# Vision tower on one core: the last stage in token x channel form behind the attention projection

## The chip, the cores and the metric

The kernel runs on one core of one Trainium2 chip. The metric is device time in microseconds; several executions are taken and their median is compared.

## What is computed

Four images of 3138 tokens with 128 channels (3136 patches of 4 x 4 and two class tokens) go through four blocks, each fed by a layer norm and added to its input. The change lies in the last two:

```python
h = h + _L1_attn_ref(_layernorm(h), w_qkv, w_proj, b_proj)   # windows of 64 tokens; per token an 8 x 8 softmax over its heads
h = h + _L1_ffn_ref(_layernorm(h), ln_scale, ln_bias, ...)
# _L1_attn_ref, last step: out.transpose(0, 2, 1, 3).reshape(B*nw, W, C) @ w_proj.T + b_proj
# _L1_ffn_ref:
flat = norm(flat) * ln_scale + ln_bias
out_shared = swiglu(flat @ shared_in_w.T) @ shared_out_w.T + shared_out_b
g_idx = argmax(flat @ group_gate_w.T + group_bias)           # one of 2 groups
topv, topi = top_k(softmax(e_logits of that group), 2)       # two of its 4 experts
h_expert = swiglu(flat @ expert_in_w.T)                      # one hidden layer of 256 for all experts
routed = cnt @ expert_out_bias
for e in range(8):
    routed = routed + comb[:, e:e+1] * (h_expert @ expert_out_weight[e].T)
return out_shared + routed
```

The transpose before the projection mixes tokens and heads inside a window, so a row of the projection's input comes from eight tokens. All of it is float32; the shares and counts are split into bf16 pieces where they pass TensorE.

## The kernel before

Three phases follow each other, each with a hand-written program for every engine; a wait is always on a semaphore. Phase A (patches, norm, state-space scan, first norms) and phase B (for each of 8 experts the 1024 best tokens, by a radix search on DVE, then gather, two matmuls and a scatter back into `h_rows`) are all but untouched. Phase C holds the last two blocks.

Phase C works on 25 groups of 512 tokens. A group passes five stages, one in each turn: L (load and row norm), A (q, k, v and the head softmax), N (projection and second norm), U (up projections and gates), X (experts). `group_turns` runs 29 turns, so in a full turn five groups are in work, and in the first and last four only some of them. Each engine has one list of steps for a turn, written out by hand at the end of `tensor` (L1710 to L1746), `scalar` (L1851 to L1872), `vector` (L2051 to L2080), `gpsimd` and `sync`. `BANK_ORDER` (L1420) gives each result of TensorE one of eight PSUM banks; `result` waits for the matmul, `taken` waits until the bank was emptied.

What a turn does:

- **A**: TensorE turns `n3`, then four matmuls make q, k and v (L1645), which ACT copies out (`qkv_copy`). POOL multiplies q with k (L2089, four of 1024 elements) and, after the softmax, the probabilities with v (L2096). DVE sums the products (`sum_scores` L1964, `sum_values` L1991) and forms the softmax (`less_top`, `probs`). The value sums of tiles 2 and 3 run in the next turn.
- **N**: TensorE turns the attention result `o` (`turn_o`, L1653), ACT copies it to `ot` (`keep_o`, L1790), SP writes it to DRAM (`heads`, L1586) and reads it back dealt out anew by eight DMAs (`dealt`, L1589). `project` (L1691) has the result as channel x token and adds the token rows `x` through four matmuls with the identity (L1695). Mean and variance run over the partitions, so they are matmuls too: `center` and `variance`. ACT and DVE finish the norm (`keep_h3`, `square`, `column_scale`, `rescale`, `affine`).
- **U**: eight up matmuls (L1613), `silu` on ACT and `hidden` on DVE give `hid`. `gates` (L1629) and nine small DVE operations (`choose_group`) pick the group.
- **X**: `choose_experts` (L2023 to L2047, 16 small DVE operations and four writes into `cc`) makes counts and shares. They are turned, split into three bf16 pieces on ACT and DVE (`keep_choice`, `split_mid`, `middle_choice`, `split_low`) and spread over the partitions by `spread` (L1672, one bf16 matmul of 512 columns per expert). DVE multiplies both halves of the hidden layer by them:

```python
dve.tensor_tensor(sc[:, k % SC_RING, :, :], hid[X % 2][:, 2:4, :],
                  tile_of(f"cb{e}", X)[:].unsqueeze(1).to_broadcast([P, 2, GW]), ALU.mult)   # scale, L1957, 1024 elements
```

and `expert` (L1680) adds two matmuls per expert into the bank ACC, where `shared` and `biases` already are. `finish` (L1900) adds the residual, and SP stores the group.

SP's list for a turn is: load `x` three groups ahead, store the last result (it waits for `finish`), then `heads` out and `dealt` in. Its weights for phase C are loaded at the start of the phase (L1573, L1574).

## Time and profile before

| | us |
|---|---|
| median of 3 runs | 2853.29 |
| lowest, highest | 2849.75, 2855.03 |
| profiled execution, own time | 2854.72 |
| its span from first to last instruction | 2852.9 |
| first weight load of phase C | 1819.9 |
| PE, DVE busy | 2417.9 (85%), 2351.7 (82%) |
| POOL, ACT busy | 1946.2 (68%), 1544.7 (54%) |
| mean granted TensorE clock | 0.934 of 2.4 GHz |

The span and the runs' times differ by under 2 us. Phase A takes about the first 1480 us, phase B until 1820, phase C the rest, some 1033 us. PE, DVE, ACT and POOL are the compute engines, SP issues DMAs. A wait is listed with the instruction that ended it. Durations of neighbouring instructions overlap a little, so start-to-start distances are shorter than the durations beside them: two DVE sums of 1024 elements take 2.33 together and 1.22 each.

### The profile page before, as it was taken

What the parts mean: (1) busy time and instruction counts of PE and PEld (TensorE: products, weight loads), DVE (VectorE), ACT (ScalarE), POOL (GpSimd) and SP (SyncE); (2) the same over time, 40 slices, a digit from 0 to 9 for tenths busy, and PEclk for the clock granted to TensorE, in tenths of its full rate; (3) what the DMA queues carried; (4) which work ended last, traced back from release to release, by engine and by line L of the source; (5) the groups of instructions that cost most, each with busy time, mean ns of one, the idle gap of its engine ahead of it and who ended that gap; (6) DMA issues with size and microseconds to landing.
All of it is one profiled execution on the core that took longest, in us unless ns stands there. A gap on an engine that the chain in (4) does not pass through costs nothing. (4 is left out here: it accounts for less than half of the span.)

```text
span 2852.9 us, 25309 instructions
## 1 busy us (share of the span) xinstructions
PE 2417.9 (85%) x6774; PEld 1128.9 (40%) x6774; DVE 2351.7 (82%) x3447; ACT 1544.7 (54%) x2598; POOL 1946.2 (68%) x1008
## 2 busy tenths in 40 slices
PE   5999999999999999999861397159999999899988
PEld 2444444444444444444321143024444444444443
DVE  2999999999999999999978522158887888888875
ACT  4777777777776777777632153134344444344332
POOL 2898898988989889898950388565555555555540
PEclk8999999999999999999975598559999999999999
DMA  2333433334333333433320043300101000011000
GB/s 75 101 120 92 124 105 113 108 95 123 103 112 106 104 118 100 124 98 110 114 82 0 20 70 56 57 22 26 30 30 30 26 28 24 26 30 30 26 23 11
DMA packets 169759, 199.28 MB, mean 70 GB/s; under 512 B 38969, under 2 KB 156946, under 8 KB 169490
## 3 DMA queue, kind: packets, MB, share of 16 engines
q1 hardware_dynamic: 158354, 189.27, 21.6%
q0 software_dynamic: 11264, 8.40, 2.2%
q8 instruction: 56, 0.92, 0.1%
q14 instruction: 85, 0.70, 0.1%
HBM read 164.37 MB, written 33.25 MB: 69 GB/s over the span
## 5 line engine op out<-in xcount | busy, mean ns | idle before, releaser
L915 POOL TENSOR_TENSOR a_hc<-a_h,a_cs 128x896 f32<-128x896 f32 (+1 forms) x448 | 859.5, 1938 | 55.8 <-DVE a_h L778 55.6
L362 PE MATMUL a_y_bank<-a_hc,a_ident 128*128 128x448 f32 (+1 forms) x1792 | 741.8, 544 | 21.8 <-DVE a_yz L798 21.2
L553 ACT ACTIVATE a_da<-a_dt,a_neg_a 128x448 f32<-128x448 f32 (+1 forms) x896 | 551.9, 631 | 296.0 <-DVE a_h L778 291.0
L778 DVE TENSOR_TENSOR_SCAN a_h<-a_da,a_h,a_dbx 128x448 f32<-128x448 f32 x528 | 582.9, 1133 | 9.5 <-ACT a_da L553 4.4
L2096 POOL TENSOR_TENSOR c_prod<-c_prob,c_qkv 128x1024 f32<-128x1024 f32 x100 | 280.8, 2848 | 272.2 <-DVE c_prob L1983 272.2
L362 PEld LDWEIGHTS a_y_bank<-a_hc,a_ident 128*128 128x128 f32 x1792 | 331.5, 190 | 326.3 <-issue 272.6
L1680 PE MATMUL c_p_ACC<-c_sc,c_w_ex 128*128 128x512 f32 x800 | 363.7, 592 | 0.0
L762 DVE TENSOR_TENSOR a_dbx<-a_dtx,a_b_bank 128x896 f32<-128x896 f32 (+1 forms) x308 | 327.3, 1063 | 16.2 <-PE a_b_bank L355 16.1
L2089 POOL TENSOR_TENSOR c_prod<-c_qkv 128x1024 f32<-128x1024 f32 x100 | 231.8, 2341 | 153.2 <-ACT c_qkv L1764 153.2
L1957 DVE TENSOR_TENSOR c_sc<-c_hid,c_p_CB 128x1024 f32<-128x1024 f32 x200 | 240.0, 1214 | 68.5 <-PE c_p_CB L1672 65.8
L903 POOL TENSOR_TENSOR a_dbp<-a_dtx,a_bs 128x896 f32<-128x896 f32 (+1 forms) x140 | 270.9, 1935 | 0.0
L778 DVE TENSOR_TENSOR_SCAN a_h<-a_da,a_h,a_dbp 128x448 f32<-128x448 f32 x240 | 263.1, 1128 | 0.0
L1680 PEld LDWEIGHTS c_p_ACC<-c_sc,c_w_ex 128*128 128x128 f32 x800 | 151.7, 190 | 182.0 <-issue 179.4
L1613 PE MATMUL c_p_W<-c_fl,c_w_up 128*128 128x512 f32 x400 | 211.3, 624 | 9.5 <-ACT c_fl L1848 8.2
L1758 ACT ACTIVATE c_act_half<-c_p_W 128x512 f32<-128x512 f32 x100 | 59.9, 599 | 251.0 <-PE c_p_W L1613 248.9
L405 PE MATMUL a_work<-a_xn,a_w_tap 128*128 128x448 f32 (+1 forms) x448 | 187.3, 552 | 3.7 <-ACT a_xn L694 3.7
L355 PE MATMUL a_b_bank<-a_bc,a_sel 128*128 128x448 bf16 (+1 forms) x308 | 110.2, 358 | 73.5 <-DVE a_dbx L762 71.5
L1385 POOL DMA_INDIRECT b_xg<-n_rows,b_index x64 | 62.3, 974 | 141.2 <-DVE b_tab L1255 122.0
L1991 DVE TENSOR_REDUCE c_o<-c_prod 128x128 f32<-128x1024 f32 x100 | 117.2, 1211 | 38.7 <-POOL c_prod L2096 38.7
L1964 DVE TENSOR_REDUCE c_score<-c_prod 128x64 f32<-128x1024 f32 x100 | 121.2, 1212 | 20.2 <-POOL c_prod L2089 18.0
L932 POOL TENSOR_TENSOR a_spl<-a_spl,a_yt 128x896 f32<-128x896 f32 (+1 forms) x28 | 58.6, 2094 | 90.3 <-DVE a_yt L805 68.0
L1764 ACT COPY c_qkv<-c_p_T 128x384 f32<-128x384 f32 x100 | 49.0, 490 | 130.7 <-PE c_p_T L1645 123.1
(304 smaller groups left out, 3718.2 us busy)
## 6 DMA issues: line engine op xcount, KB each, us to landing
a_cs<-c_rows SPq DMA_DIRECT2D x96, 896.0 KB, 5.2
a_bs<-c_rows SPq DMA_DIRECT2D x24, 1120.0 KB, 5.6
a_cs<-c_rows SPq DMA_DIRECT2D x16, 900.0 KB, 4.4
c_x<-h_rows SPq DMA_DIRECT2D x25, 256.0 KB, 2.7
heads<-c_ot SPq DMA_DIRECT2D x25, 256.0 KB, 2.3
c_dealt<-heads SPq DMA_DIRECT2D x200, 32.0 KB, 1.9
rolled<-c_res SPq DMA_DIRECT2D x25, 256.0 KB, 2.1
h_rows<-a_th SPq DMA_DIRECT2D x24, 224.0 KB
```

Of the source, the lines that this page charges most:

```text
L362: pe.matmul(y_bank[:, d, 0:g.w], ident[:], hc[:, (g.i * NS + n) % HC_RING, d, 0:g.w], start=(n == 0), stop=(n == NS - 1)).then_inc(s_sum, 1)
L405: mm = pe.matmul(tile_of(use, p)[:, 0:w], w_tap[:, j, d * P:(d + 1) * P], xn[:, j:j + w], start=(j == 0), stop=(j == KC - 1))
L553: act.activation(da[:, k % DA_RING, 0:g.w], dt[g.slot][:, d, 0:g.w], ACT.Exp, scale=neg_a[:, d * NS + n:d * NS + n + 1]).then_inc(s_da, 1)
L762: dve.tensor_tensor(dbx[:, k % DBX_RING, :, 0:g.w], dtx[g.slot][:, :, 0:g.w], b_bank[:, 0:g.w].unsqueeze(1).to_broadcast([P, 2, g.w]), ALU ...
L778: dve.tensor_tensor_scan(h[:, n, d, 0:g.w], da[:, (g.i * 2 * NS + k) % DA_RING, 0:g.w], x, state, ALU.mult, ALU.add).then_inc(s_scan, 1)
L903: pool.tensor_tensor(dbp[:, k % DBP_RING, :, 0:g.w], dtx[g.slot][:, :, 0:g.w], bs[:, POOL_STATES.index(n), 0:g.w].unsqueeze(1).to_broadcas ...
L915: pool.tensor_tensor(hc[:, (q.i * NS + n) % HC_RING, :, 0:q.w], h[:, n, :, 0:q.w], cs[:, n % C_RING, 0:q.w].unsqueeze(1).to_broadcast([P, ...
L1613: end(f"up{m}", U, pe.matmul(p[:], w_up[:, m * P:(m + 1) * P], fl[U % 2][:], start=True, stop=True))
L1680: mm = pe.matmul(p[:], w_ex[:, i, e * D:(e + 1) * D], sc[:, k % SC_RING, i, :], start=False, stop=(e == E1 - 1 and i == 1))
L1957: dve.tensor_tensor(sc[:, k % SC_RING, :, :], hid[X % 2][:, 2:4, :], tile_of(f"cb{e}", X)[:].unsqueeze(1).to_broadcast([P, 2, GW]), ALU.mu ...
L2089: pool.tensor_tensor(prod[j][:].rearrange("p (h g d) -> p h g d", h=NH, g=NH), q.rearrange("p (h d) -> p h d", d=DH).unsqueeze(2).to_broad ...
L2096: pool.tensor_tensor(prod[j][:].rearrange("p (h d g) -> p h d g", h=NH, g=NH), prob[:, j * NH:(j + 1) * NH, :].unsqueeze(2).to_broadcast([ ...
```

## The change

Phase C keeps its five stages, groups and eight banks. From `project` on, everything is token x channel, with tokens on the partitions:

- `project` is one bf16 matmul for the bias and four float32 matmuls of 128 columns that have `dealt` as the stationary side. The residual is added by DVE (`add_rows`) from SBUF. Mean and variance come from `bn_stats` and `bn_aggr` on DVE, the scaling is four ACT instructions with a scale and a shift per row (`norm_rows2`), and TensorE turns the result (`turn_n2`) for the up matmuls. `center`, `variance`, `square`, `column_scale`, `rescale`, `keep_h3` and the identity matmuls go.
- `ex(n)` multiplies one tile of 128 tokens of the hidden layer, now the stationary side, with the weights of four experts at once, 512 moving columns; two of them cover a tile. There are still 16 matmuls of 512 columns in a turn. The shares, now one number per row, are applied as the two banks E0 and E1 are emptied: `by_act` (0 to 3) with four ACT instructions of 128 columns each, `by_dve` (4 to 7) with one DVE instruction of 512. `spread`, `scale` and both splits go. The bias matmul is four bf16 matmuls of 128 columns.
- POOL adds the two halves of each tile (`add_experts`, 512 elements, four per turn) between its products. DVE sums the four pairs, the residual and ACC in `total`, two `tensor_reduce` per group whose summed axis has a step of 128 elements. ACT copies ACC out (`keep_acc`).
- The windows are dealt so that a tile holds the same places of eight windows: `x` is loaded by four DMAs instead of one, `keep_o` writes runs of eight elements, and the output is token x channel.
- `qkv_copy(j)` waits for the value product of its own tile only. SP stores the last result after it has issued `heads`.
- The constants of phase C get their own memory beside phase B's and are loaded during it. POOL's fills at the start of phase B wait for DVE's first five operations there.

```diff
+            if e == 2:
+                progs["c_load"](sp)
             need(sp, s_out, 2 * (e - 1))
...
+            if r == 6:
+                progs["c_clear"](dve)
             decide(r, limit[0])
...
+        pool.wait_ge(s_dve, progs["n_high"])
         pool.memset(ones[:], 1.0).then_inc(s_fill, 1)
         pool.memset(zeros[:], 0).then_inc(s_fill, 1)
...
+    def load(sp):
+        for dst, name in ((k.ident, "ident"), (k.w_qkv, "w_qkv"), (k.w_proj, "w_proj"), (k.w_up, "w_up"),
+                          (k.w_gate, "w_gate"), (k.cols, "cols_c"), (k.w_so, "w_so"), (k.w_ex, "w_ex"),
+                          (k.earlier, "earlier"), (k.later, "later"), (k.pick, "picks_p")):
+            sp.dma_start(dst[:], a[name]).then_inc(k.s_in, 16)
+        sp.dma_start(k.gate_b[:], a["gate_b"].rearrange("o n -> (o n)").partition_broadcast(P)).then_inc(k.s_in, 16)
+        sp.wait_ge(k.s_const, 1)
+        for first in PARTS:
+            sp.dma_start(k.bias10[first:first + NBIAS, :], a["bias10"]).then_inc(k.s_in, 16)
...
+        free = result(eng, f"ex{n}", c)
+        rows = sc[:, entry % SC_RING, half * EG:(half + 1) * EG, :]
+        got = tile_of(f"ex{n}", c)[:].rearrange("p (e d) -> p e d", e=EG)
+        return rows, got, shares[:, c % 2, j, half * EG:(half + 1) * EG], free
+
...
+            def load():
+                if L is not None:
+                    if L >= 3:
+                        taken(sp, "proj", L - 3)
+                    rows = h_rows[L * GW + SHIFT:(L + 1) * GW + SHIFT, :].rearrange("(w n) d -> n w d", n=WIN)
+                    for j in range(GT):
...
+                    taken(sp, "o", N)
+                    sp.dma_start(heads[N % 2], ot[:]).then_inc(s_heads[N % 2], 16)
+
+            def heads_in():
...
+                        sp.dma_start(dealt[s][j * DH:(j + 1) * DH, :, :],
+                                     heads[s][:, j, :].rearrange("(h d) c -> d h c", d=DH)).then_inc(s_dealt[s], 16)
+
+            load()
...
+                    for j in range(GT):
+                        for k in range(2):
+                            pe.matmul(p[:, j * D:(j + 1) * D], hid[X % 2][:, k, j * P:(j + 1) * P], w_so[:, k, :],
+                                      start=(j == 0 and k == 0), stop=False, skip_group_check=True)
...
+                    for j in range(GT):
+                        mm = pe.matmul(p[:, j * D:(j + 1) * D], c_b[0:KB, j * P:(j + 1) * P], bias_b[0:KB, :],
+                                       start=False, stop=True, skip_group_check=True)
+                    end("acc", X, mm)
...
+                    j, half = n // 2, n % 2
+                    if n == 0:
+                        taken(pe, "up7", X)
+                    p = begin(f"ex{n}", X)
                     for i in range(2):
-                        mm = pe.matmul(p[:], w_ex[:, i, e * D:(e + 1) * D], sc[:, k % SC_RING, i, :], start=False,
-                                       stop=(e == E1 - 1 and i == 1))
...
+                        mm = pe.matmul(p[:], hid[X % 2][:, 2 + i, j * P:(j + 1) * P],
+                                       w_ex[:, i, half * EG * D:(half + 1) * EG * D], start=(i == 0), stop=(i == 1))
+                    end(f"ex{n}", X, mm)
...
+                    pe.matmul(p[:], pick_b[0:KB, :], bias_b[0:KB, :].unsqueeze(1).to_broadcast([KB, GT, D]),
+                              start=True, stop=False, skip_group_check=True)
...
                     for j in range(GT):
-                        mm = pe.matmul(p[:, j * P:(j + 1) * P], x[N % 3][:, j, :], ident[:], start=False,
-                                       stop=(j == GT - 1), skip_group_check=True)
+                        rows = dealt[N % 2][:, 2 * j:2 * j + 2, :].rearrange("p h c -> p (h c)")
+                        mm = pe.matmul(p[:, j * D:(j + 1) * D], rows, w_proj[:], start=False, stop=True,
+                                       skip_group_check=True)
...
+            shared()
+            ex(0)
+            turn_n3()
             up(0)
+            ex(1)
             up(1)
-            turn_n3()
+            qkv_mm(0)
+            qkv_mm(1)
             up(2)
+            qkv_mm(2)
             up(3)
-            qkv_mm(0)
             turn_o()
-            qkv_mm(1)
+            ex(2)
+            gates()
             up(4)
+            qkv_mm(3)
             turn_choice()
-            qkv_mm(2)
-            shared()
-            gates()
+            ex(3)
+            up(5)
             biases()
-            spread(0)
-            qkv_mm(3)
-            spread(1)
-            up(5)
+            up(6)
             project()
-            up(6)
-            spread(2)
-            expert(0)
-            spread(3)
-            expert(1)
-            spread(4)
-            center()
-            expert(2)
-            expert(3)
-            spread(5)
-            variance()
-            spread(6)
-            expert(4)
-            spread(7)
+            ex(4)
+            ex(5)
+            ex(6)
             up(7)
-            expert(5)
-            expert(6)
-            expert(7)
+            ex(7)
+            turn_n2()
 
```

ACT, DVE and POOL:

```diff
+                    need(act, s_pv, (A - 1) * GT + j + 1)
...
+                    act.copy(ot[:].rearrange("p j (a w) -> p a j w", w=NW),
+                             tile_of("o", N)[:].rearrange("p (a j w) -> p a j w", j=8, w=NW)
...
+                    rows, got, part, free = evict(act, X, n)
+                    for e in range(EG):
+                        i = act.activation(rows[:, e, :], got[:, e, :], ACT.Copy, scale=part[:, e:e + 1])
+                    i.then_inc(free, 1)
...
             silu(3)
+            by_act(3)
             exp_table()
-            keep_h3()
+            gate_exp()
             score_exp()
-            square()
+            row_scale2()
+            keep_acc()
             row_scale()
+            norm_rows2()
+            silu_table()
             norm_rows()
-            column_scale()
-            gate_exp()
-            silu_table()
             affine()
...
+            dve.wait_ge(s_add, c * GT + 2 * k + 2)
             if c >= 2:
...
+            dve.tensor_reduce(res[c % 2][:, 2 * k:2 * k + 2, :],
+                              parts[s][:, 2 * k:2 * k + 2, :, :].rearrange("p j e d -> p j d e"), AX.X, ALU.add
+                              ).then_inc(s_sum, 1)
...
+                    rows, got, part, free = evict(dve, X, n)
+                    dve.tensor_tensor(rows, got, part.unsqueeze(2).to_broadcast([P, EG, D]), ALU.mult).then_inc(free, 1)
...
+                    free = result(dve, "proj", N)
+                    h3 = parts[N % SUM_RING][:, :, OF_ROW, :]
+                    dve.tensor_tensor(h3, tile_of("proj", N)[:].rearrange("p (j d) -> p j d", j=GT), x[N % 3][:], ALU.add
+                                      ).then_inc(free, 1)
+                    taken(dve, "proj", N)
+                    for j in range(GT):
+                        i = dve.bn_stats(stats2[:, j, :], h3[:, j, :])
...
+            choose_experts()
+            total_last(0)
             sum_values(N, 2)
+            hidden(0)
             sum_values(N, 3)
-            hidden(0)
-            choose_experts()
+            sum_scores(0)
+            total_last(1)
+            sum_scores(1)
+            stats_of()
             hidden(1)
-            finish_last()
-            split_mid()
-            sum_scores(0)
-            split_low()
-            sum_scores(1)
+            sum_scores(2)
             choose_group()
-            sum_scores(2)
-            scale(0)
-            scale(1)
-            scale(2)
-            stats_of()
             sum_scores(3)
-            scale(3)
             less_top()
+            add_rows()
+            by_dve(4)
             probs()
-            scale(4)
             hidden(2)
-            scale(5)
+            less_mean2()
+            by_dve(5)
             less_mean()
-            scale(6)
-            scale(7)
             hidden(3)
-            rescale()
+            by_dve(6)
+            by_dve(7)
             sum_values(A, 0)
...
+            def add_experts(j):
+                if X is not None:
+                    n = X * GT + j
+                    taken(pool, f"ex{2 * j}", X)
+                    taken(pool, f"ex{2 * j + 1}", X)
+                    need(pool, s_sum, 2 * (X - SUM_RING) + j // 2 + 1)
+                    rows = sc[:, n % SC_RING, :, :]
+                    pool.tensor_tensor(parts[X % SUM_RING][:, j, 0:EG, :], rows[:, 0:EG, :], rows[:, EG:E1, :], ALU.add
+                                       ).then_inc(s_add, 1)
...
+            score_products(0)
+            score_products(1)
+            score_products(2)
+            add_experts(0)
+            score_products(3)
+            value_products(0)
+            value_products(1)
+            add_experts(1)
+            add_experts(2)
+            value_products(2)
+            value_products(3)
+            add_experts(3)
```

How the lists stand now. PE, middle of a full turn, before: the twelve rows that begin with the turning of `o` and end just ahead of the projection (L1691).

```order
L1653 MATMUL c_p_M<-c_ident,c_o 128x128 x4
L1645 MATMUL c_p_T<-c_w_qkv,c_nt 128x384
L1613 MATMUL c_p_W<-c_fl,c_w_up 128x512
L1638 MATMUL c_p_M<-c_ident,c_cc 104x128 x4
L1645 MATMUL c_p_T<-c_w_qkv,c_nt 128x384
L1660 MATMUL c_p_ACC<-c_hid,c_w_so 128x512 x2
L1629 MATMUL c_p_R<-c_w_gate,c_fl 128x10 x4
L1665 MATMUL c_p_ACC<-c_c_t,c_bias 128x512
L1672 MATMUL c_p_CB<-c_c_b,c_sel_e 128x512
L1645 MATMUL c_p_T<-c_w_qkv,c_nt 128x384
L1672 MATMUL c_p_CB<-c_c_b,c_sel_e 128x512
L1613 MATMUL c_p_W<-c_fl,c_w_up 128x512
```

The same stretch of the changed kernel, from the turning of `o` up to the projection itself (L1784, L1789; L1777 is `ex`, L1734 the turned choice, L1766 the biases):

```order
L1749 MATMUL c_p_T<-c_ident,c_o 128x128 x4
L1777 MATMUL c_p_E<-c_w_ex,c_hid 128x512 x2
L1725 MATMUL c_p_R<-c_w_gate,c_fl 128x10 x4
L1708 MATMUL c_p_W<-c_fl,c_w_up 128x512
L1741 MATMUL c_p_T<-c_w_qkv,c_nt 128x384
L1734 MATMUL c_p_M<-c_ident,c_cc 74x128 x4
L1777 MATMUL c_p_E<-c_w_ex,c_hid 128x512 x2
L1708 MATMUL c_p_W<-c_fl,c_w_up 128x512
L1766 MATMUL c_p_ACC<-c_bias_b,c_c_b 128x128 x4
L1708 MATMUL c_p_W<-c_fl,c_w_up 128x512
L1784 MATMUL c_p_T<-c_bias_b,c_pick_b 128x512
L1789 MATMUL c_p_T<-c_w_proj,c_dealt 128x128 x4
```

Between the turned `o` and the projection stood three q, k, v matmuls, two up matmuls, `shared`, the gates, the biases and two `spread`; now there are four expert matmuls, three up matmuls, one of q, k, v, the gates and the biases.

ACT, start of a turn, before (L1758 `silu`, L1769 `keep_n3`, L1764 `qkv_copy`, L1790 `keep_o`):

```order
L1758 ACTIVATE c_act_half<-c_p_W 128x512
L1769 COPY c_nt<-c_p_T 128x512
L1764 COPY c_qkv<-c_p_T 128x384
L1758 ACTIVATE c_act_half<-c_p_W 128x512
L1790 COPY c_ot<-c_p_M 128x64x8
L1764 COPY c_qkv<-c_p_T 128x384
```

The same stretch of the changed kernel (L1850 `keep_n3`, L1929 `by_act`, L1839 `silu`, L1845 `qkv_copy`, L1865 `keep_o`):

```order
L1850 COPY c_nt<-c_p_T 128x512
L1929 ACTIVATE c_sc<-c_p_E,c_shares 128x128 x4
L1839 ACTIVATE c_act_half<-c_p_W 128x512
L1845 COPY c_qkv<-c_p_T 128x384
L1845 COPY c_qkv<-c_p_M 128x384
L1839 ACTIVATE c_act_half<-c_p_W 128x512
L1845 COPY c_qkv<-c_p_T 128x384
L1929 ACTIVATE c_sc<-c_p_E,c_shares 128x128 x4
L1865 COPY c_ot<-c_p_T 128x8x8x8
```

Between `keep_n3` and `keep_o` stood one copy and one `silu`; now there are three copies, two `silu` and two evictions of four instructions each.

DVE, from the last sum of scores to the probabilities, changed kernel (L2034 `sum_scores`, L2068 to L2076 `add_rows`, L2029 `by_dve`, L2049 to L2053 `probs`):

```order
L2034 TENSOR_REDUCE c_score<-c_prod 128x64
L2041 TENSOR_REDUCE c_top<-c_score 128x32
L2043 TENSOR_TENSOR c_score<-c_score,c_top 128x256
L2068 TENSOR_TENSOR c_parts<-c_p_T,c_x 128x4x128
L2072 BN_STATS c_stats<-c_parts 128x6 x4
L2076 BN_AGGR c_mv<-c_stats 128x2 x4
L2029 TENSOR_TENSOR c_sc<-c_p_E,c_shares 128x512
L2049 TENSOR_REDUCE c_denom<-c_expo 128x32
L2051 RECIPROCAL c_denom<-c_denom 128x32
L2053 TENSOR_TENSOR c_prob<-c_expo,c_denom 128x256
```

Before, one `scale` stood ahead of `less_top` and nothing between `less_top` and `probs`; six instructions of the N stage's norm (the addition, the four `bn_stats` with their four `bn_aggr`) and one eviction now stand between them.

## Rows read from the trace of the kernel before

**Rows 1.** Busy time by stage, last stage's full groups (busy us per engine, clock, DMA)

```profile
1967.00:2723.00 756.00, 703.86 (x2080) 336.13 (x2080) 637.95 (x1361) 307.79 (x561) 410.70 (x160) 0.98 0.09 28
```

**Rows 2.** Timeline of POOL, score products: start, length, name, idle before

```profile
1840.59 9.20 POOL L2089 TENSOR_TENSOR c_prod<-c_qkv 128x1024 f32<-128x1024 f32 x4 [22.61 <-ACT c_qkv L1764]
...
1966.99 6.94 POOL L2089 TENSOR_TENSOR c_prod<-c_qkv 128x1024 f32<-128x1024 f32 x3 [4.26 <-ACT c_qkv L1764]
...
2270.13 6.95 POOL L2089 TENSOR_TENSOR c_prod<-c_qkv 128x1024 f32<-128x1024 f32 x3 [4.27 <-ACT c_qkv L1764]
...
2306.87 6.95 POOL L2089 TENSOR_TENSOR c_prod<-c_qkv 128x1024 f32<-128x1024 f32 x3 [4.26 <-ACT c_qkv L1764]
...
2723.05 6.94 POOL L2089 TENSOR_TENSOR c_prod<-c_qkv 128x1024 f32<-128x1024 f32 x3 [4.26 <-ACT c_qkv L1764]
```

**Rows 3.** Chain of work that ended last, one group of turns (2300 to 2347)

```profile
2304.57 0.20 DVE c_p_R L2024
...
2308.54 0.60 DVE c_hid L1932
...
2310.17 2.32 DMA heads<-c_ot
...
2317.75 2.04 PE c_p_M L1691 x2
```

**Rows 4.** Timeline of PE in a turn at the full clock

```profile
2280.97 1.10 PE L1691 MATMUL c_p_M<-c_dealt,c_w_proj 128*128 128x512 f32 x2 [2.04 <-DMA c_dealt<-heads]
2281.90 1.05 PE L1695 MATMUL c_p_M<-c_ident,c_x 128*128 128x128 f32 x8
2282.79 1.02 PE L1613 MATMUL c_p_W<-c_fl,c_w_up 128*128 128x512 f32 x2
2283.65 0.38 PE L1672 MATMUL c_p_CB<-c_c_b,c_sel_e 104*128 104x512 bf16 x1
2283.87 1.88 PE L1680 MATMUL c_p_ACC<-c_sc,c_w_ex 128*128 128x512 f32 x4
2285.59 0.38 PE L1672 MATMUL c_p_CB<-c_c_b,c_sel_e 104*128 104x512 bf16 x1
```

**Rows 5.** Timeline of PE in the next turn, half clock after the gap

```profile
2317.75 2.04 PE L1691 MATMUL c_p_M<-c_dealt,c_w_proj 128*128 128x512 f32 x2 [2.08 <-DMA c_dealt<-heads]
...
2321.23 1.02 PE L1613 MATMUL c_p_W<-c_fl,c_w_up 128*128 128x512 f32 x2
```

**Rows 6.** Groups by line and shape, 2100 to 2650: PE (busy, mean ns, idle before)

```profile
L1629 PE MATMUL c_p_R<-c_w_gate,c_fl 128*128 128x10 f32 x112 | 13.4, 247 | 0.0
...
L1653 PE MATMUL c_p_M<-c_ident,c_o 128*128 128x128 f32 x60 | 9.0, 273 | 0.0
```

**Rows 7.** The same view: DVE

```profile
L1957 DVE TENSOR_TENSOR c_sc<-c_hid,c_p_CB 128x1024 f32<-128x1024 f32 x116 | 139.6, 1213 | 34.1 <-PE c_p_CB L1672 32.1
...
L1964 DVE TENSOR_REDUCE c_score<-c_prod 128x64 f32<-128x1024 f32 x56 | 67.8, 1211 | 1.4
...
L1932 DVE TENSOR_TENSOR c_hid<-c_act_half,c_p_W 128x512 f32<-128x512 f32 x60 | 40.7, 679 | 0.0
...
L1912 DVE BATCH_NORM_STATS2 c_stats<-c_x 128x6 f32<-128x128 f32 x56 | 12.1, 278 | 0.0
```

**Rows 8.** The same view: ACT

```profile
L1834 ACT ACTIVATE c_n<-c_x,c_shift,c_rstd 128x128 f32<-128x128 f32 x60 | 24.7, 483 | 50.6 <-DVE c_shift L1925 50.6
...
L1790 ACT COPY c_ot<-c_p_M 128x512 f32<-128x512 f32 x15 | 15.9, 1062 | 0.0
...
L1769 ACT COPY c_nt<-c_p_T 128x512 f32<-128x512 f32 x15 | 8.8, 587 | 10.5 <-PE c_p_T L1620 10.5
```

**Rows 9.** Timeline at the start of the last stage: SP and DVE

```profile
1819.89 0.33 SPq L1573 DMA_DIRECT2D c_ident<-in_ident  x1
...
1832.59 0.68 DVE L1912 BATCH_NORM_STATS2 c_stats<-c_x 128x6 f32<-128x128 f32 x3
```

**Rows 10.** Timeline at the start of phase B: DVE beside POOL

```profile
1487.61 1.93 DVE L1121 TENSOR_SCALAR b_x<-b_x 128x785 f32<-128x785 f32 x1
```

402 lines of the change are left out of this document (209 added, 193 removed), and 10 rows, old and new, of the table BANK_ORDER.

## The prediction

> **What bounds the kernel now.** I read the busy times by stage first. In phase C's full turns PE is busy 703.9 of 756 us, 93%, at 0.98 of the full clock, DVE 84%, POOL 54%, ACT 41% [rows 1]. So PE is nearly the bound and DVE is close behind. POOL's timeline gives the turn: from the fifth group's first score product at 1966.99 to the last group's at 2723.05 are 20 turns, 37.8 us each; the four turns while the pipeline fills take 126.4 together, and from 2723.05 to the end are 129.8 [rows 2]. The turn from 2270.13 takes 36.7 [rows 2].
>
> The chain of waits shows a circle through all engines: the value sums, the choice of experts on DVE (about 4.0, from 2304.57 to 2308.54), the last result, then `heads` at 2310.17 and the projection at 2317.75, 7.58 later [rows 3]. PE stands 2.04 us in front of the projection, and in the shorter turn that is its one long gap [rows 4]. In the next turn it stands 2.08 and then runs at half clock (1.2 instead of 2.4 GHz): projection and identity matmuls take 3.48 from start to start instead of 1.82, 1.7 more [rows 4, 5]. A turn is thus 36.74 - 2.04 = 34.7 of PE work, 2.0 of waiting, and on average 1.1 for such slow stretches and the like. Two limits must be followed in the change: PE's work, and the circle through the DRAM round trip.
>
> **The change on PE.** Start to start, a float32 matmul of 512 columns is 0.86, a bf16 one 0.22, four float32 ones of 128 columns 0.89, and an expert's pair 1.72 [rows 4]. Four turned tiles are 9.0 / 15 = 0.60, the gates 13.4 / 14 = 0.96 [rows 6]. Removed: eight `spread` 8 x 0.22 = 1.76, mean, variance and bias 3 x 0.86 = 2.58, the identity matmuls 0.89: 5.23. Added: `turn_n2` 0.60; the bf16 biases, four of 128 columns, at least one `spread` (0.22) and at most 0.89, taken as 0.3; the projection goes from 0.93 to 0.22 + 0.89 = 1.11, `shared` from 1.72 to eight of 128 columns, 1.78: together 1.14. The 16 expert matmuls of 512 columns stay 16. PE's work becomes 34.7 - 5.23 + 1.14 = 30.6.
>
> **The change on DVE.** Busy 638 / 20 = 31.9 a turn [rows 1]. Removed: eight `scale` at 1.21 = 9.7 and four operations of 512 (two splits, `finish`, `rescale`) at 0.68 = 2.7 [rows 7]. Added: four `by_dve` at 0.68 = 2.7; `add_rows` 0.68 plus the four statistics 0.86 (12.1 / 14) plus some 0.4 for the aggregates; and two `total`. A sum of 1024 elements takes 1.21 and an operation of 512 takes 0.68 [rows 7], so 1536 elements take 1.75 if their step of 128 elements costs nothing; 3.5 for both. New: 31.9 - 12.4 + 8.1 = 27.6.
>
> **ACT and POOL.** `by_act` is 16 instructions of 128 columns a turn. The nearest row, `norm_rows`, has 128 columns with a scale and a shift per row: four take 24.7 / 15 = 1.65 [rows 8]. From below, a quarter of a copy of 512 columns (0.59) is 0.15 each; I take 0.41, since a short instruction is mostly fixed cost. That is 6.6, with 1.65 for `norm_rows2` and about 1.1 for the rest; six operations of 512 at about 0.6 go. ACT: 15.4 + 9.4 - 3.7 = 21.1. POOL gets four additions of 512 elements at 1.15 (four of 1024 take 9.20 [rows 2]): 20.5 + 4.6 = 25.1. Neither is a bound by sum.
>
> For `by_act` the Trainium skill (ScalarE: Activation LUTs, What ACT_TABLE_LOAD costs) states 186 ns plus 0.833 per column, 93 more for each per-row operand, and 93 of overlap between neighbours. For one operand that would be about 0.29 instead of 0.41, 0.5 less per eviction; two evictions stand on the path below, so by it a turn would be 1.0 shorter and the sum 20 us lower. No run here shows a one-operand instruction yet.
>
> **The wait at the projection.** `keep_o` now stands behind `by_act(1)`, which starts as PE turns `o`: 1.65, then `keep_o` 1.06 [rows 8], a hand-over of 0.1, then 7.58 to the projection [rows 3]: 10.4. PE has ahead of it, by the excerpt: turned `o` 0.60, two expert pairs 3.44, gates 0.96, three ups 2.58, one q, k, v some 0.65 (three quarters of 0.86), choice 0.60, biases 0.3, bf16 bias 0.22: 9.35. A gap of 1.0 stays. SP's store no longer stands ahead of `heads`, and DVE is through with `total` before the round trip ends. With the 1.1 of slow stretches the turn is 30.6 + 1.0 + 1.1 = 32.7.
>
> **The circle** is checked by the same prices. From the end of `probs`: two `hidden`, three `by_dve`, two value sums and the wait for the last up, 6.8; the choice 4.1; `by_act(0)` 1.65; `silu`, copy, up, `silu`, copy about 3.2; `by_act(1)` and `keep_o` 2.7; round trip 7.6; projection 1.2; `add_rows` 1.9; `by_dve(4)` 0.6; `probs` 1.3. These are 31.1, and some 14 hand-overs of 0.1 make 32.5. Both limits fall together, which never runs without friction, so I take **33.0**. What is new here: `probs`, for which POOL waits, stands behind `add_rows`, hence behind the DRAM round trip.
>
> **The sum.** 20 turns x (37.8 - 33.0) = 96. Start: the first `x` load can go at 1819.9, where the first weight went; four loads and a landing later, about 1824.2, DVE can begin instead of at 1832.59 [rows 9]: 8. The weights land during phase B, whose DMA queues idle while DVE searches; without that cover these 8 come back. Fill: the first of four turns has no expert or projection work, the others gain at about half the full rate: 8. Drain: one full turn's gain and three at half: 12. POOL's fills leave DVE's first pass in phase B alone, 1.93 for 785 elements [rows 10] where 0.68 per 512 lets expect 1.0: with its neighbour 2, between 0 and 3. The 15 loads inside phase B's queue cost nothing, as two experts' weights are queued ahead. Together 126: 2854.7 - 126 = **2728**. The profiled execution is 1.4 above the median.
>
> **Rivals.**
> 1. *The strided sums.* `total` reads with a step of 512 bytes. DVE shows no such row; on ACT, `keep_o`, which writes with a step, takes 1.06 against 0.59 for a plain copy of the same size, 1.8 times [rows 8]. At that ratio `total` takes 3.2, 2.8 more a turn, and all of it lies on the circle, one in front of the value sums and one in front of the scores: turn 35.8, gain 40 + 28, time 2787. DVE's contiguous sums speak neither way. The Trainium skill (SBUF - State Buffer, Door 1: The DMA port swizzle) says that every access that crosses into another 16-byte line pays a penalty; that is this rival. Chance 0.18.
> 2. *The round trip hides.* If evictions on ACT are short, PE does not stand in front of the projection and keeps the full clock: 30.6 and some 0.6 of friction, turn 31.2, gain 132 + 31, time 2692. Chance 0.13.
> 3. *Slower: PE starves on two banks.* E0 and E1 are freed by `by_act`, which waits for the choice of experts; `silu(0)` and three copies stand behind it on ACT, so `up(2)` and `qkv_mm(2)` wait too. If PE stands over 2 us at three places of a turn, each costs 2.1 and 1.7 at half clock [rows 4, 5]: 30.6 + 11.4 = 42, 20 x 4.2 = 84 lost against 28 gained elsewhere, time 2911. It decides from a turn of 39.2 on. Against it: by the prices above the choice ends about when PE reaches `up(1)`. Chance 0.06.
> 4. *It does not do what it says*: the expert matmuls are as many and as wide as before, so if the small matmuls cost more than in rows 4 the gain shrinks to nothing only with all the rest. Within 0.2%: 0.03.
>
> The forecast's own case, a turn between 32 and 35, gives 2700 to 2771 and has 0.60. The range 2692 to 2790 takes in rivals 1 and 2. 0.2% (6 us) is about what a measurement of this kernel tells from no change. Faster 0.91, same 0.03, slower 0.06.
>
> **What would show it.** Right: score products 33 apart; PE busy near 30.6 a turn; four `by_act` 1.65 together; `total` 1.75; PE's longest gap about 1 us in front of L1789, ended by the `dealt` DMA; first statistics of phase C near 1824. Wrong: `total` over 2.5; PE waiting for ACT in front of `ex` or `up(2)`; a granted clock under 0.95 in the full turns; POOL waiting over 6 us for `probs`.

## The result, and the profile after

The kernel before took 2852.9 us (median of 4 runs) and the changed kernel 2759.7 (2758.0 to 2762.6, 4 runs). The ratio is 0.9668, with a 95% interval from 0.9651 to 0.9686: 3.3% faster. The forecast was 2728, the range 2692 to 2790. The profiled run has a span of 2759.4.

First the busy times of the 20 full turns, between the fifth and the last group's first score product (us busy and number of instructions of PE, PEld, DVE, ACT and POOL, then the granted clock, the DMA share and GB/s). This answers to [rows 1].

```profile
1950.89:2653.00 702.11, 612.57 (x2181) 309.57 (x2180) 676.66 (x1441) 365.33 (x901) 507.32 (x240) 1.00 0.11 30
```

PE works 612.6 / 20 = 30.6 us a turn. DVE is busy 96% of the time, 33.8 a turn, and is now the engine nearest to the bound; before it was PE [rows 1]. The granted clock is 1.00 where it was 0.98.

POOL's timeline gives the turn, as [rows 2] did:

```profile
1835.07 9.19 POOL L2174 TENSOR_TENSOR c_prod<-c_qkv 128x1024 f32<-128x1024 f32 x4 [15.12 <-ACT c_qkv L1845]
...
1950.89 6.94 POOL L2174 TENSOR_TENSOR c_prod<-c_qkv 128x1024 f32<-128x1024 f32 x3 [1.05 <-ACT c_qkv L1845]
...
2198.44 6.96 POOL L2174 TENSOR_TENSOR c_prod<-c_qkv 128x1024 f32<-128x1024 f32 x3 [1.02 <-ACT c_qkv L1845]
...
2217.52 5.57 POOL L2183 TENSOR_TENSOR c_prod<-c_prob,c_qkv 128x1024 f32<-128x1024 f32 x2 [7.76 <-DVE c_prob L2053]
...
2233.36 6.97 POOL L2174 TENSOR_TENSOR c_prod<-c_qkv 128x1024 f32<-128x1024 f32 x3 [1.01 <-ACT c_qkv L1845]
...
2653.00 6.97 POOL L2174 TENSOR_TENSOR c_prod<-c_qkv 128x1024 f32<-128x1024 f32 x3 [1.02 <-ACT c_qkv L1845]
```

The account of the two traces, from these starts and those of [rows 2]. The first score product comes 5.5 us earlier (1840.59 to 1835.07). The four turns of the fill take 115.8 for 126.4, a gain of 10.6. The 20 full turns take 702.1 for 756.1, 35.1 each for 37.8, a gain of 54.0. From the last group's first score product to the end are 106.4 for 129.8, a gain of 23.4. Together 93.5.

Now DVE's and ACT's groups in the same stretch (busy, mean ns | idle before):

```profile
L1988 DVE TENSOR_REDUCE c_res<-c_parts 128x256 f32<-128x1536 f32 x41 | 116.1, 2832 | 0.0
...
L1929 ACT ACTIVATE c_sc<-c_p_E,c_shares 128x128 f32<-128x128 f32 x320 | 91.2, 372 | 90.5 <-DVE c_shares L2135 66.2 <-PE c_p_E L1777 24.3
...
L2084 DVE SCALAR_TENSOR_TENSOR c_shift<-c_mv,c_rstd 128x4 f32<-128x4 f32 x20 | 47.6, 2379 | 0.0
L2014 DVE SCALAR_TENSOR_TENSOR c_shift<-c_mv,c_rstd 128x4 f32<-128x4 f32 x20 | 45.1, 2253 | 0.0
...
L1789 PE MATMUL c_p_T<-c_w_proj,c_dealt 128*128 128x128 f32 x160 | 24.0, 295 | 15.0 <-DMA c_dealt<-heads 15.0
...
L1865 ACT COPY c_ot<-c_p_T 128x512 f32<-128x512 f32 x20 | 11.7, 585 | 27.1 <-PE c_p_T L1749 27.1
```

`total` (L1988) takes 2.83 us, where the prediction had 1.75. The two multiplications of the row means by the row scales, `less_mean2` and `less_mean` (L2084, L2014), take 2.38 and 2.25 us for four numbers in a row. The second was there in the kernel before too, with a median of 0.17. DVE's timeline shows where the time goes:

```profile
2217.02 0.42 DVE L2053 TENSOR_TENSOR c_prob<-c_expo,c_denom 128x256 f32<-128x256 f32 x1
2217.36 0.68 DVE L2023 TENSOR_TENSOR c_hid<-c_act_half,c_p_W 128x512 f32<-128x512 f32 x1
2217.95 2.38 DVE L2084 SCALAR_TENSOR_TENSOR c_shift<-c_mv,c_rstd 128x4 f32<-128x4 f32 x1
2220.25 0.68 DVE L2029 TENSOR_TENSOR c_sc<-c_p_E,c_shares 128x512 f32<-128x512 f32 x1
2220.85 2.25 DVE L2014 SCALAR_TENSOR_TENSOR c_shift<-c_mv,c_rstd 128x4 f32<-128x4 f32 x1
```

POOL's pair of value products runs from 2217.52 for 5.57, so 2.79 each: the first ends at 2220.3, the second at 2223.1. `less_mean2` ends at 2220.33 and `less_mean` at 2223.10. Each stands until the product that is running is over. The Trainium skill (SBUF — State Buffer, Who interferes with whom) says that a VectorE instruction with both inputs in SBUF contends with a GpSimd instruction that reads SBUF, and that the pair of ports which they share is an exclusive lock; the rows agree. The changed kernel has a check of its own: in the one turn in which `less_mean` (L2014) came just as a product ended (1904.8), the same instruction took 0.15:

```profile
1904.74 0.15 DVE L2014 SCALAR_TENSOR_TENSOR c_shift<-c_mv,c_rstd 128x4 f32<-128x4 f32 x1
```

In the kernel before the same instruction happened to start just where one product ended: three instructions of fixed length lay between the probabilities and it, and POOL's first product is as long as they are. These are the two rows of the kernel before, DVE's and POOL's (four products in 11.26, so the first ends at about 2294.16):

```profile
2294.04 0.18 DVE L1925 SCALAR_TENSOR_TENSOR c_shift<-c_mv,c_rstd 128x4 f32<-128x4 f32 x1
```

```profile
2291.34 11.26 POOL L2096 TENSOR_TENSOR c_prod<-c_prob,c_qkv 128x1024 f32<-128x1024 f32 x4 [10.57 <-DVE c_prob L1983]
```

The median gave no warning, but the longest did. In two of the 25 turns, while the pipeline filled, the instruction began inside a product and took 1.27 and 1.88. The second ended at 1918.78, with POOL's first product (three in 8.33 from 1915.96 on):

```profile
1916.90 1.88 DVE L1925 SCALAR_TENSOR_TENSOR c_shift<-c_mv,c_rstd 128x4 f32<-128x4 f32 x1 [0.42 <-ACT c_rstd L1809]
```

```profile
1915.96 8.33 POOL L2096 TENSOR_TENSOR c_prod<-c_prob,c_qkv 128x1024 f32<-128x1024 f32 x3 [9.16 <-DVE c_prob L1983]
```

The waits of the changed kernel in the full turns, in total us, times and longest, over 20 turns:

```profile
POOL c_prod L2183 <- DVE c_prob L2053: 159.0, 20, 10.3
...
PE c_p_E L1777 <- DVE c_sc L2029: 33.2, 20, 1.8
...
PE c_p_W L1708 <- DVE c_hid L2023: 20.5, 20, 1.0
PE c_p_W L1708 <- ACT c_act_half L1839: 18.6, 21, 0.9
...
PE c_p_T L1789 <- DMA c_dealt<-heads: 15.0, 20, 2.2
```

These four waits of PE are 1.7, 1.0, 0.9 and 0.75 a turn. With 30.6 of work they make 35.0 of the turn's 35.1. The first two are for DVE. The prediction had only the last. POOL waits 8.0 a turn for the probabilities, which the prediction named as a sign against it from 6 on. The sign is a weak one: POOL waited 11.6 a turn for them in the kernel before, and 6.5 in run 3, whose turn is shorter than the forecast.

### The profile page after: what moved, and what is told of

Read it like the earlier page. It is cut to its first block and busy times, and to the rows that moved or that the text cites. A ratio compares the mean times of both kernels' runs of the same rounds, so it can differ in the third digit from the quotient of the medians.

```text
span 2759.4 us, 26470 instructions
## 1 busy us (share of the span) xinstructions
PE 2294.0 (83%) x6899; PEld 1098.8 (40%) x6899; DVE 2382.7 (86%) x3555; ACT 1616.4 (59%) x3023; POOL 2068.2 (75%) x1108
## 5 line engine op out<-in xcount | busy, mean ns | idle before, releaser
L1777 PE MATMUL c_p_E<-c_w_ex,c_hid 128*128 128x512 f32 x800 | 375.4, 599 | 38.3 <-DVE c_sc L2029 36.3
L1708 PE MATMUL c_p_W<-c_fl,c_w_up 128*128 128x512 f32 x400 | 217.4, 627 | 50.1 <-DVE c_hid L2023 29.9
L1777 PEld LDWEIGHTS c_p_E<-c_w_ex,c_hid 128*128 128x128 f32 x800 | 142.1, 191 | 197.3 <-issue 124.2
L1929 ACT ACTIVATE c_sc<-c_p_E,c_shares 128x128 f32<-128x128 f32 x400 | 113.9, 372 | 118.0 <-DVE c_shares L2135 87.2
L2195 POOL TENSOR_TENSOR c_parts<-c_sc 128x512 f32<-128x512 f32 x100 | 126.8, 1279 | 51.4 <-ACT c_sc L1929 35.8
L1988 DVE TENSOR_REDUCE c_res<-c_parts 128x256 f32<-128x1536 f32 x50 | 141.1, 2826 | 0.0
L2034 DVE TENSOR_REDUCE c_score<-c_prod 128x64 f32<-128x1024 f32 x100 | 121.5, 1215 | 20.4 <-POOL c_prod L2174 19.6
```

The source lines that it names most:

```text
L1708: end(f"up{m}", U, pe.matmul(p[:], w_up[:, m * P:(m + 1) * P], fl[U % 2][:], start=True, stop=True))
L1777: mm = pe.matmul(p[:], hid[X % 2][:, 2 + i, j * P:(j + 1) * P], w_ex[:, i, half * EG * D:(half + 1) * EG * D], start=(i == 0), stop=(i == 1))
L1988: dve.tensor_reduce(res[c % 2][:, 2 * k:2 * k + 2, :], parts[s][:, 2 * k:2 * k + 2, :, :].rearrange("p j e d -> p j d e"), AX.X, ALU.add). ...
```

## The experiments

Each run was compared with the kernel before on the same chip. The chips differ between the rows (the kernel before took 2846.4 to 2852.9), so the ratios compare better than the times. A turn is, as above, a twentieth of the way from the fifth to the last group's first score product, and busy times are those of that stretch over 20.

| run | median us | ratio (95%) | turn | DVE | first score product |
|---|---|---|---|---|---|
| changed kernel | 2759.7 | 0.9668 (0.9651 to 0.9686) | 35.11 | 33.8 | 1835.1 |
| 1 means in PSUM | 2707.1 | 0.9493 (0.9472 to 0.9513) | 33.07 | 30.3 | 1829.8 |
| 2 sum in line | 2716.7 | 0.9530 (0.9511 to 0.9550) | 33.02 | 31.7 | 1829.9 |
| 3 both | 2682.4 | 0.9407 (0.9387 to 0.9426) | 31.85 | 28.0 | 1831.4 |
| 4 slots last | 2702.0 | 0.9477 (0.9458 to 0.9496) | 32.69 | 28.8 | 1828.8 |
| 5 old heads | 2700.1 | 0.9464 (0.9441 to 0.9486) | 32.61 | 28.8 | 1829.4 |
| 6 weights late | 2765.1 | 0.9694 (0.9671 to 0.9717) | 34.94 | 33.8 | 1839.6 |
| 7 statistics behind | 2703.0 | 0.9475 (0.9453 to 0.9496) | 32.61 | 28.7 | 1830.4 |
| 8 two moves | 2702.2 | 0.9473 (0.9451 to 0.9494) | 32.63 | 28.7 | 1829.8 |
| 9 adds in the gap | 2696.8 | 0.9467 (0.9451 to 0.9483) | 32.35 | 29.6 | 1828.2 |
| 10 the same and two moves | 2697.1 | 0.9467 (0.9451 to 0.9483) | 32.41 | 29.7 | 1829.4 |
| 11 the gap alone | 2768.2 | 0.9712 (0.9696 to 0.9728) | 35.58 | 34.4 | 1829.1 |
| 12 fifth bank by ACT | 2688.3 | 0.9438 (0.9420 to 0.9456) | 32.06 | 28.2 | 1830.3 |

### Run 1: the means in PSUM

```diff
-  dve.scalar_tensor_tensor(out=shift[:], in0=mv[:, :, 0], scalar=-1.0, in1=rstd[:],
-                           op0=ALU.mult, op1=ALU.mult).then_inc(s_shift, 1)
+  dve.tensor_scalar(neg, mv[:, :, 0], -1.0, None, ALU.mult).then_inc(s_neg, 1)
+  dve.wait_ge(s_neg, L + 1)
+  dve.tensor_tensor(shift[:], neg, rstd[:], ALU.mult).then_inc(s_shift, 1)
```

(`neg` lies in the PSUM bank R; `less_mean2` in the same way.)

> The changed kernel, but each of the two small operations that multiply the row means by the row scales (less_mean and less_mean2) first copies the negated means to a PSUM bank and then multiplies with one input in PSUM and one in SBUF. THEORY A (VectorE is the bound, and these two operations, with both inputs in SBUF, stand until GpSimd's value product is over): the second of the two falls from a median of 2.3 us to about 0.2, VectorE's busy time falls from 33.8 to about 29.8 us a turn (4.3 less, some 0.3 for the copies more), and the turn from 35.1 to some 32.5 (TensorE's 30.6 and 1.8 of waits for ScalarE and the dealt heads are left). Over 20 turns and the fill that is 50 to 65 us: 2695 to 2710. RIVAL B (the stall is cover: the chain of the row norm waits for something else anyway, and TensorE's waits are set by the round trip through DRAM): the two operations get shorter, the time stays within 8 us of 2760. RIVAL C (it is not the port: these small operations take 2.3 us because ScalarE's result arrives late and the record holds the wait): they stay at 2.3 us whichever memory the means are in, time unchanged.

DVE's timeline of run 1 at the same place, and POOL's:

```profile
2224.87 0.42 DVE L2056 TENSOR_TENSOR c_prob<-c_expo,c_denom 128x256 f32<-128x256 f32 x1
...
2225.81 0.16 DVE L2087 TENSOR_SCALAR c_p_R<-c_mv 128x4 f32<-128x4 f32 x1
2226.01 0.16 DVE L2089 TENSOR_TENSOR c_shift<-c_p_R,c_rstd 128x4 f32<-128x4 f32 x1
...
2226.72 0.15 DVE L2016 TENSOR_SCALAR c_p_R<-c_mv 128x4 f32<-128x4 f32 x1
2226.91 0.16 DVE L2018 TENSOR_TENSOR c_shift<-c_p_R,c_rstd 128x4 f32<-128x4 f32 x1
```

```profile
2225.38 5.64 POOL L2187 TENSOR_TENSOR c_prod<-c_prob,c_qkv 128x1024 f32<-128x1024 f32 x2 [7.57 <-DVE c_prob L2056]
```

The value products run again from 2225.38, and the small operations take 0.16 in the midst of them. Rival C is out: the instruction no longer stands once the means lie in PSUM. The edit also makes two instructions of one, but the kind of instruction is not what counts: the same kind takes 0.15 and 0.17 above when no product holds it, and in run 9 a `tensor_tensor` with two SBUF inputs is held too. DVE falls by 3.6 us a turn, the turn by 2.0, and the ratio from 0.9668 to 0.9493, 50 us. Rival B is out too. Of the 52 us between the two profiles 41 lie in the 20 turns, 5.2 in an earlier first score product (see run 6), the rest in fill and drain. Theory A asked for a turn of 32.5; it is 33.1.

### Run 2: the sum in line

```diff
-  parts[s][:, 2 * k:2 * k + 2, :, :].rearrange("p j e d -> p j d e")
+  parts[s][:, 2 * k:2 * k + 2, :, :].rearrange("p j e d -> p j (e d)")
+                                    .rearrange("p j (d e) -> p j d e", e=SLOTS)
```

> The changed kernel, but the sum over the six slots (total) reads the same 1536 elements in the order in which they lie in memory, not 512 bytes apart; the sums that it gives are of other elements, so the output is not the reference's. THEORY A (the stride costs 1.1 us each, and VectorE is the bound): total falls from 2.83 to about 1.75 us, VectorE's 33.8 us a turn to about 31.6, the turn from 35.1 to about 33; time 2710 to 2725. RIVAL B (what is late is not VectorE's): total 1.75, time within 8 us of 2760. RIVAL C (a reduce of 1536 elements over six costs 2.8 us however it reads): total stays at 2.8 and the time at 2760.

```profile
L1988 DVE TENSOR_REDUCE c_res<-c_parts 128x256 f32<-128x1536 f32 x40 | 69.8, 1744 | 0.0
```

1.74 us against 2.83, for the same 1536 elements. The price 1.75 was right for a sum in line, and the step of 512 bytes costs 1.09 each time, 2.2 a turn. The turn falls by 2.1. Rivals B and C fall.

### Run 3: both

> Both edits of the last two runs in one kernel (again sums of other elements, so the output is not the reference's). THEORY A: VectorE falls to 27.6 us a turn, which is what the prediction gave it, so that TensorE and the circle of heads, projection and row norm set the turn: if the prediction's step for those was right, the turn is 32 to 33 and the two gains do not add (2695 to 2705, not 2650). RIVAL D (the turn follows VectorE's work all the way down, TensorE's 30.6 being hidden): turn 31, 2665 to 2680.

```profile
1943.54:2580.53 636.99, 610.10 (x2181) 308.28 (x2180) 560.72 (x1481) 365.84 (x901) 506.94 (x241) 1.00 0.12 33
```

DVE 28.0, where the prediction had 27.6. The two gains together are 3.3 a turn, not 4.1: something else begins to bind, and theory A was right in kind. But the turn is 31.85, below its 32 to 33, and the time 2682, below 2695. Rival D, a turn of 31, went too far.

### Run 4: slots innermost

```diff
-  parts = [sb(f"parts{s}", [P, GT, SLOTS, D]) ...
+  parts = [sb(f"parts{s}", [P, GT, D, SLOTS]) ...
```

(All readers and writers index accordingly. The means are in PSUM as in run 1.)

> The means in PSUM as in the first run, and the parts laid out with the six slots innermost, so that the sum reads what lies in line and is right; who writes the slots (GpSimd's adds, ScalarE's copy of the shared sums, VectorE's add of the rows) now writes 24 bytes apart, and two readers read so. THEORY E (only a reduce's strided read costs): total 1.75, the writers unchanged, time as in the third run. RIVAL F (writes at a stride cost as much as reads at one): add_experts grows from 1.28 us by 0.3 to 1 us each, add_rows and the row statistics by 0.3 each; GpSimd goes from 25.4 to some 28 us a turn, VectorE ends at about 28.5, and the time is 2700 to 2715, no better than the first run.

```profile
L2199 POOL TENSOR_TENSOR c_parts<-c_sc 128x512 f32<-128x512 f32 x81 | 103.1, 1286 | 0.0
...
L1990 DVE TENSOR_REDUCE c_res<-c_parts 128x256 f32<-128x1536 f32 x41 | 71.5, 1744 | 0.0
...
L1907 ACT ACTIVATE c_n<-c_parts,c_shift,c_rstd 128x128 f32<-128x128 f32 x80 | 43.2, 612 | 16.5 <-DVE c_shift L2089 16.5
...
L2075 DVE BATCH_NORM_STATS2 c_stats<-c_parts 128x6 f32<-128x128 f32 x80 | 25.0, 375 | 0.7
...
L2071 DVE TENSOR_TENSOR c_parts<-c_p_T,c_x 128x512 f32<-128x512 f32 x20 | 21.5, 1073 | 0.9 <-PE c_p_T L1791 0.9
L1924 ACT COPY c_parts<-c_p_ACC 128x512 f32<-128x512 f32 x20 | 21.1, 1056 | 0.0
```

POOL writes 24 bytes apart at no cost (1286 ns for 1281). ACT and DVE do not: the copy of the shared sums goes from 567 to 1056 ns, the add of the rows from 685 to 1073, the statistics that read so from 281 to 375, `norm_rows2` from 482 to 612. That gives back 0.8 of the 2.2 us on DVE. Each theory is half right. The 2702 is 0.2% below run 1, which the ratios don't tell apart, and 0.7% above run 3, which they do.

### Run 5: the round trip taken away

```diff
+  of = max(N - 1, 0)
-  pe.wait_ge(s_dealt[N % 2], (N // 2 + 1) * (16 * 8))
+  pe.wait_ge(s_dealt[of % 2], (of // 2 + 1) * (16 * 8))
```

> The fourth run's kernel (means in PSUM, slots innermost, turn 32.7), but the projection reads the heads that were dealt a turn earlier, so that it never waits for the present round trip through DRAM; the output is not the reference's. THEORY A (the round trip is nearly hidden: the trace of the fourth run shows TensorE standing 0.4 us a turn before the projection): the turn falls by 0.3 to 0.5, the time by 6 to 10 us, to about 2694. RIVAL G (the circle over heads, projection and row norm is what still sets the turn, as the prediction had it with 32.5 us, and the short wait only looks small because everything else has lined up with it): the turn falls by 1 us or more, time at most 2680.

The time is that of run 4 within what can be measured, and the turn falls by 0.1, less than theory A's 0.3 too. Rival G falls: the trip through DRAM is hidden at this turn. PE's wait did not even vanish but moved, to the bank that DVE empties. Its longest wait there was 0.9 in run 4 and is 1.5 now:

```profile
PE c_p_E L1779 <- DVE c_sc L2033: 30.1, 20, 1.5
```

### Run 6: the weights late

> The changed kernel, but the loads of the last stage's weights and tables are issued where the kernel before issued them, at the stage's start ahead of the rows of x, and no longer behind the second expert's weights in the stage before. THEORY A (the preload is worth what the prediction gave it): the first row statistics come 8 us or more later after the last scatter than they do in the changed kernel (4.3 us behind the issue of x there), nothing else moves, and the time is 2766 to 2773. THEORY H (the preload also cost the stage before some 5 us, by a stall of ScalarE and VectorE near 1640 us that the kernel before does not have): that stall is gone in this run, and the time comes out near 2762. RIVAL I (the loads are hidden behind the chain x, row statistics, first products): time within 3 us of 2760 with the stall still there.

The start of the last stage is read from the last scatter's issue on POOL to the first statistics of `x` on DVE. That is 16.2 us in the kernel before, 7.6 in the changed kernel, 17.8 in this run. The preload is worth 10.2 against this run, which differs in nothing else, and 8.5 against the kernel before; the prediction had 8. The changed kernel also lost something in phase B, and this run does not. There the last scatter issues at 1818.40, in the kernel before at 1816.42, and here at 1812.79. The loss lies at one place, in ACT's timeline of the changed kernel:

```profile
1637.06 0.69 ACT L1308 ACTIVATE b_ot<-b_p_o,b_b 128x512 f32<-128x512 f32 x1 [3.25 <-remote]
1643.40 0.69 ACT L1308 ACTIVATE b_ot<-b_p_o,b_b 128x512 f32<-128x512 f32 x1 [5.65 <-remote]
```

and the same two instructions in run 6:

```profile
1633.60 0.69 ACT L1306 ACTIVATE b_ot<-b_p_o,b_b 128x512 f32<-128x512 f32 x1 [1.13 <-PE b_p_o L1365]
1637.04 0.69 ACT L1306 ACTIVATE b_ot<-b_p_o,b_b 128x512 f32<-128x512 f32 x1 [2.75 <-PE b_p_o L1365]
```

By the profile PE's matmuls for these two end at 1634.9 and 1638.3, but the profile models these ends. The trace's semaphore events have PE's signals for them at 1637.04 and 1643.37, 2.1 and 5.0 later, and ACT began 0.02 to 0.03 after each. In the 221 other instances that the 14 profiles record the signal comes 0.01 after the modelled end, and ACT begins as soon after it. So ACT was not late, PE's signal was; DVE, SP and POOL waited behind it (POOL 4.1). The time, 2765, lies between what the theories gave. So theory H's observation is right. Its cause is not: runs 1 to 5 and 7 to 12 all load the weights in phase B, and in all of them the last scatter issues between 1811.6 and 1814.7, with no such wait. The preload alone does not bring the stall. It stands in the one profiled execution of the changed kernel; whether its other executions have it is not shown, nor what held PE's signal (the "remote" in the row is only the profile's guess). Between the profiles some 5 of the 52 us of run 1 are thus not that edit's, and likewise in the other runs.

### Runs 7 and 8: DVE's order

```diff
   add_rows()
   by_dve(4)
+  row_stats()                # taken out of add_rows
...
-  stats_of()
   hidden(1)
+  stats_of()                 # run 8 only
```

> The fourth run's kernel, but VectorE empties the expert bank (by_dve 4) between the add of the rows and their statistics, not behind the statistics. THEORY J (TensorE stands 0.87 us a turn because that bank is emptied behind 1.6 us of statistics, and that is what is left of the turn above TensorE's work): the wait goes, the row norm comes 0.7 later and costs nothing yet; turn 32.7 to 32.0, time about 2686 to 2690. RIVAL K (the row norm's chain, statistics, scale, norm, transpose, gates, is as tight as the bank): what is won at the bank is lost at the norm, time 2698 to 2704.

> The last run's kernel, and the second product of the hidden halves (hidden 1) ahead of the statistics of x, since TensorE stands 0.5 us a turn for it. THEORY J: turn 32.7 to about 31.5, a further 0.4 to 0.5 below the last run; time 2675 to 2682. RIVAL K: VectorE's order only moves the wait to the next bank; within 4 us of the last run.

Both stay at run 4's time. Theory J falls, and rival K's times hold, though the wait moved to other places than the row norm. In run 7 PE's wait for the bank is gone and 0.8 in front of the next up projection, for DVE's `hidden`, is new. In run 8 0.4 (the median) before the projection has become 1.2:

```profile
2217.83 1.16 PE L1791 MATMUL c_p_T<-c_w_proj,c_dealt 128*128 128x128 f32 x8 [1.16 <-DMA c_dealt<-heads]
...
2224.91 1.13 PE L1710 MATMUL c_p_W<-c_fl,c_w_up 128*128 128x512 f32 x2 [0.78 <-DVE c_hid L2026]
```

A DVE with 12% idle can still be the engine that everything hangs on, because what is asked of it comes in one stretch.

### Runs 9, 10 and 11: POOL's adds in its own gap

```diff
-  add_experts(0)
   score_products(3)
+  add_experts(0)
+  add_experts(1)
   value_products(0)
   value_products(1)
-  add_experts(1)
```

> The fourth run's kernel, with GpSimd's order changed: all four score products first, then the adds of the first two pairs of expert results, then the value products (before, one of these adds stood ahead of the last score product and one behind the first two value products). THEORY L (what sets the turn once VectorE is relieved is GpSimd's own row: 25.4 us of work and the 7.1 to 7.2 us in which it waits for the probabilities, 32.6 together, which is the turn of the fourth, fifth, seventh and eighth run; the two adds, 2.6 us, fit in that wait): the wait for the probabilities falls to about 4.6 and the turn to TensorE's 30.6 and some 0.5 to 1 of waits, 31.1 to 31.6; time 2665 to 2680. RIVAL M (GpSimd's row only lines up with the others; VectorE's order or the round trip sets the turn): the wait stays at 7 us, or what is won there turns up in front of the other products; time 2697 to 2704.

> The eighth run's kernel (both moves on VectorE) with GpSimd's order of the last run. THEORY L: the moves, worth nothing while GpSimd's row set the turn, take away part of what is left above TensorE's work; turn 30.8 to 31.2, time 2660 to 2670, that is 3 to 10 us less than the last run. RIVAL M: the moves still give nothing, and the round trip of the heads, for which this order waited 1.2 us a turn, is what is left: equal to the last run or up to 10 us slower.

> The changed kernel with GpSimd's order alone. THEORY A (in the changed kernel VectorE is the bound, 33.8 of 35.1 us, so GpSimd's order is worth little there): turn 34.5 to 35.1, time within 12 us of 2760, and some of that from where the stalled small operations fall against GpSimd's. RIVAL N (GpSimd's row was the bound in the changed kernel too, and relieving VectorE only helped because GpSimd waits for VectorE's probabilities): turn 32.5 to 33, time 2705 to 2720.

```profile
2210.23 1.29 POOL L2199 TENSOR_TENSOR c_parts<-c_sc 128x512 f32<-128x512 f32 x1
2213.29 1.28 POOL L2199 TENSOR_TENSOR c_parts<-c_sc 128x512 f32<-128x512 f32 x1 [1.78 <-issue]
2219.35 5.65 POOL L2187 TENSOR_TENSOR c_prod<-c_prob,c_qkv 128x1024 f32<-128x1024 f32 x2 [4.78 <-DVE c_prob L2056]
```

```profile
2218.15 1.98 PE L1779 MATMUL c_p_E<-c_w_ex,c_hid 128*128 128x512 f32 x4 [1.75 <-DVE c_sc L2032]
```

```profile
2212.95 0.42 DVE L2044 TENSOR_REDUCE c_top<-c_score 128x32 f32<-128x256 f32 x1
2213.41 1.44 DVE L2046 TENSOR_TENSOR c_score<-c_score,c_top 128x256 f32<-128x256 f32 x1
```

POOL's wait for the probabilities fell from 7.2 to 4.8, but the second add waits 1.8 itself, until ACT has emptied `ex(3)` (2213.16), and PE stands 1.75 for the bank. The turn falls by 0.3 only; theory L falls, and the ratios of runs 4 and 9 can't be told apart. The last rows show the port a second time. The subtraction of the score maxima has two SBUF inputs. It takes 0.42 as long as POOL stands idle and 1.44 here: it ends at 2214.85, 0.28 after the add that began at 2213.29 and took 1.28. Run 10 equals run 9, so rival M holds there as well. Run 11 answers for the changed kernel itself: its turn grows by 0.5, beyond theory A's 35.1, and POOL waits 2.2 and 2.0 us for ACT's copies of q, k, v, where it waited 1.0 and 0.8. POOL's order was not its bound, and rival N falls.

### Run 12: the fifth bank by ACT

```diff
   score_exp()
+  by_act(4)
   row_scale2()
...
-  by_dve(4)
```

(Also `add_experts(0)` behind `score_products(3)`; the rest is run 4.)

> The fourth run's kernel (means in PSUM, slots innermost) with two edits: the fifth expert bank (ex4) is emptied by ScalarE, between the exponentials of the scores and the scale of the rows, where ScalarE stands for 2.0 to 2.3 us a turn, and no longer by VectorE; and GpSimd adds the first pair of results behind the last score product, the second pair where it did before (in the ninth run both stood in front of the probabilities, and the second collided with VectorE's subtraction of the score maxima, 1.44 us there for 0.42). THEORY O (VectorE's row between the last score sum and the probabilities is what sets the turn: whatever is taken out of that stretch shortens GpSimd's wait and TensorE's wait for the bank together): VectorE has 0.67 us less ahead of the probabilities, TensorE waits under 0.3 us for that bank; turn 31.4 to 31.9, time 2672 to 2685. RIVAL P (the next thing in line takes it: ScalarE, now 20.3 us a turn, is late with the norm's scale or with the halves of the hidden rows): turn 32.2 to 32.7, time 2692 to 2702.

```profile
1946.09:2587.25 641.16, 610.23 (x2181) 309.43 (x2180) 564.51 (x1461) 405.86 (x982) 507.95 (x241) 1.00 0.12 33
```

```profile
2219.87 5.66 POOL L2187 TENSOR_TENSOR c_prod<-c_prob,c_qkv 128x1024 f32<-128x1024 f32 x2 [6.64 <-DVE c_prob L2057]
```

This is the fastest kernel that computes all of the reference: 2688.3, a ratio of 0.9438, against 0.9668 of the changed kernel; by the ratios some 66 us less. The turn falls by 0.63 from run 4's, about the 0.67 taken from DVE between the last score sum and the probabilities. Turn and time lie between theory O's upper ends (31.9, 2685) and rival P's lower ones (32.2, 2692). As two edits went in together, their shares are not told apart; the other one moves an add of POOL's, and moving two of them gave 0.3 in run 9, whose ratio touches this one's interval. POOL's 25.4 of work and its wait of 6.6 fill the 32.06, PE's 30.5 leaves 1.5 of it.

## Why the prediction was right, and where it was not

- **PE's work** was forecast at 30.6 a turn and is 30.6. The count of what goes and what comes held.
- **The strided sums.** "1536 elements take 1.75 if their step of 128 elements costs nothing" is a step that failed: 2.83. Rival 1 held the case at 3.2. The truth lies between, 2.2 a turn on DVE. Run 2 shows that it is the step's price alone.
- **What no step held** is the larger miss. `less_mean2` is new and stands in no term of DVE's sum; `less_mean` was left at what it took before, 0.17. They take 4.6 together, and run 1, with the turn in which one of them took 0.15, shows that both inputs being in SBUF beside POOL's products is the cause. The forecast's 27.6, plus 2.2 and 4.5, is 34.3; measured 33.8. The step that failed is thus "New: 31.9 - 12.4 + 8.1 = 27.6". From it followed that DVE could be left out of the limits.
- **The turn.** Forecast 33.0, measured 35.1. In run 3, where both prices are gone, it is 31.85. So without them the turn is below the forecast, by about the 1.1 of slow-clock stretches that the prediction kept while the granted clock is 1.00. What remained above PE's work in run 3 is 1.35. The circle through the round trip, set at 32.5, was too long, since run 3 runs below it and run 5 shows that the trip is hidden.
- **The wait at the projection** was forecast at 1.0 and is 0.75 (median 0.42). The others, 3.6 for DVE and ACT, are those of a late DVE.
- **ACT.** `by_act` was priced at 1.65 per eviction and takes 1.14, 0.28 for each of the four, as the row below shows; they begin 0.25 apart and take 0.37 each. The figure of the Trainium skill's page (ScalarE: Activation LUTs, What ACT_TABLE_LOAD costs), 0.29, would give 1.17, an estimate, and was the nearer one. `keep_o` was priced at 1.06 and takes 0.59. It now writes runs of eight elements, which no run separates from the rest of the edit. ACT is busy 18.3 a turn, not 21.1, and nothing came of it, because ACT is not the bound. POOL was forecast at 25.1 and is busy 25.4.

```profile
2211.56 1.13 ACT L1929 ACTIVATE c_sc<-c_p_E,c_shares 128x128 f32<-128x128 f32 x4
```

- **Start, fill, drain.** The preload was worth 8.5, forecast 8, and some 5 of it was lost again by the stall in phase B. With POOL's fills out of the way the first four computing operations of DVE in phase B (from `b_level` to `b_key`) take 2.5 until the next begins instead of 5.6, a gain of 3.1 where the forecast had 2, at most 3. The pass of [rows 10], priced at 1.0, takes 0.57 (the row below). The fill gave 10.6 for 8. The drain gave 23.4 for 12. In the kernel before the draining turns still took as long as full ones: the results' stores are issued at 2725.95, 2763.84 and 2801.71, 37.9 apart. In the changed kernel they are at 2660.40, 2692.25 and 2719.02, 31.9 and 26.8 apart. "One full turn's gain and three at half" was too low.

```profile
1486.81 0.57 DVE L1123 TENSOR_SCALAR b_x<-b_x 128x785 f32<-128x785 f32 x1
```

- **The sum.** The forecast gain was 126, and 93.5 came (profile against profile): 20 turns gave 42 less than forecast, start and phase B together some 4.5 less, fill and drain 14 more. The time was right only within the range, which was wide for other reasons (rivals 1 and 2). The turn of 35.1 lies just outside the forecast's own case, 32 to 35. By the prediction's own sum it would be 2771; the profiled 2761 is lower because fill and drain gave more, and that was luck. The side, "faster", rested on PE's work, which held.
- **Rivals.** Rival 1 had the right place and too high a price. Rival 2 (turn 31.2, time 2692) is near run 3 (31.85, 2682) and not the changed kernel. Rival 3 is visible in small: PE's waits for two banks and the hidden halves, 3.6 a turn together, none over 1.8, and most of it for DVE rather than ACT.

Open stay what held PE's signals near 1640 us, and which of the tied rows (POOL's wait for the probabilities, DVE's stretch ahead of them, PE's bank) holds the turn at 32.

## What to carry to other kernels

Before a duration from the old trace is taken over for a small VectorE operation with two SBUF inputs, look at what GpSimd runs at that moment in the new order: a row of 0.17 us can become the rest of a 2.8 us product, and one operand in PSUM undoes it. Price a reduction by how far apart it reads, and before the slots are laid in line for the reader, price the writers too. Where several engines were within 10% of each other, a reorder mostly moved a wait: runs 7 to 10 gave 0.1 to 0.3 a turn. The largest step, 0.63 in run 12, took work off DVE's crowded stretch, though with a reorder beside it. Look at the longest instance of an instruction and not at its median alone.

## What the runs showed of the hardware

- A VectorE multiplication of 128 x 4 numbers took 2.25 to 2.38 us, each time until GpSimd's running instruction was over, 0.15 in the turn in which it began as one ended, and 0.16 with one input in PSUM.
- A sum over six slots 512 bytes apart took 1.62 times as long as one in line (2.83 and 1.74 us for 1536 elements).
- Writing float32 24 bytes apart cost ScalarE 1.86 times (567 to 1056 ns), VectorE 1.57 times (685 to 1073), and GpSimd nothing (1281 to 1286).
- TensorE's signals for two results came 2.1 and 5.0 us after the ends that the profile gives their matmuls (at 1637.04 and 1643.37), in one profiled execution. The 221 others of the same kind that the 14 profiles record came 0.01 after; ScalarE began 0.02 to 0.03 behind each. What held the two is not shown.
